# Batches of 4, 4, 3, 3 and 2 units, moved bias products, unread matmuls in waits, and no barrier between the samples and the experts

## What is computed

```python
qkv = src @ in_proj_w.T + in_proj_b
attn = softmax(einsum('sbhd,tbhd->bhst', q, k) * scale)   # over the samples
x = ln(src + (attn @ v) @ out_w.T + out_b)
probs = softmax(x @ gate_w.T + gate_b)
topv, topi = top_k(probs, 2)
for e in range(8):
    h = relu(tok @ w1[e].T + b1[e]) @ w2[e].T + b2[e]
    moe_out = moe_out + combine[:, e:e+1] * h
return ln(x + moe_out)
```

## Time and profile before

| | |
|---|---|
| time of 3 runs | 1171.24 us median (1170.41 to 1176.53) |
| the profiled execution | 1174.04 us, span 1172.3 us |
| mean granted TensorE clock | 0.971 |
| PE busy | 1103.8 us, 94% |
| DVE, POOL, ACT busy | 774.1, 522.6, 430.1 us |
| chain that ended last | PE 53%, issue 21%, DVE 14%, ACT 5%, POOL 4%, DMA 2% |

### The profile page before, as it was taken

How to read it: one execution, slowest core, us unless ns; L and a number is a source line. 1 busy time by engine, 2 the same in 40 slices (tenths; PEclk the granted TensorE clock), 3 DMA queues, 4 the chain that set the end, 5 groups by cost and what they waited for, 6 DMA issues and landing times.

```text
span 1172.3 us, 21067 instructions
## 1 busy us (share of the span) xinstructions
PE 1103.8 (94%) x7531; PEld 927.0 (79%) x7531; DVE 774.1 (66%) x1711; ACT 430.1 (37%) x890; POOL 522.6 (45%) x505
## 2 busy tenths in 40 slices
PE   9999999999899997999987999999999989989997
PEld 5888888886777765988986999999998678775565
DVE  5899889998887546888851222222222898887785
ACT  3545533335556411121112222222222455553466
POOL 6554224447776121768766111100254756531343
PEclk9999999999999997999977999999999999998999
DMA  6999700001000110000045422311221200000001
GB/s 221 398 394 388 265 1 1 19 7 71 17 1 1 28 75 1 1 2 28 34 143 201 158 108 107 108 38 38 63 81 39 62 10 10 1 1 2 0 28 46
DMA packets 44182, 93.61 MB, mean 80 GB/s; under 512 B 3885, under 2 KB 17998, under 8 KB 41414
## 3 DMA queue, kind: packets, MB, share of 16 engines
q1 hardware_dynamic: 35702, 62.24, 14.8%
q0 software_dynamic: 7104, 29.14, 6.9%
q10 hardware_dynamic: 1296, 1.18, 0.3%
HBM read 39.02 MB, written 51.51 MB: 77 GB/s over the span
## 4 chain that ended last, share of the span: by engine, by line
PE 53%; issue 21%; DVE 14%; ACT 5%; POOL 4%; DMA 2%; POOLq 1%; SPq 1%; PEldq 0%; DVEq 0%; PEld 0%; ACTq 0%
PE PS L2393 11%; PE PS L2403 11%; PE PS L1100 6%; PE PS L1078 3%; PE PS L1113 3%; PE PS L1068 2%; DVE scr L1459 2%; PE PS L1633 2%; PE PS L1026 2%; DVE scr L1485 2%; PE PS L1795 1%; POOL big L686 1%; DVE big L1372 1%; PE PS L1107 1%; PE PS L1023 1%
## 5 line engine op out<-in xcount | busy, mean ns | idle before, releaser
L2426 ACT ACTIVATE scr<-PS,W 128x128 f32<-128x128 f32 x148 | 53.5, 367 | 192.0 <-PE PS L2393 190.9
L2393 PEld LDWEIGHTS PS<-scr 128*128 128x128 f32 x992 | 118.2, 194 | 5.0 <-issue 1.8
L2393 PE MATMUL PS<-scr 128*128 128x128 f32 x992 | 120.2, 279 | 1.3 <-ACT scr L2421 1.3
L2403 PE MATMUL PS<-scr 128*128 128x256 f32 x496 | 112.2, 379 | 0.0
L718 POOL TENSOR_TENSOR scr<-scr,small 128x1232 f32<-128x1232 f32 x32 | 72.0, 2251 | 81.3 <-DVE small L469 81.0
L2456 DVE TENSOR_SCALAR scr<-PS,W 128x128 f32<-128x128 f32 x148 | 51.3, 350 | 82.2 <-PE PS L2393 82.2
L2403 PEld LDWEIGHTS PS<-scr 128*128 128x128 f32 x496 | 91.8, 190 | 11.2
L859 ACT ACTIVATE big<-PS 128x512 f32<-128x512 f32 x144 | 73.7, 524 | 73.0 <-PE PS L1078 72.6
L2462 DVE TENSOR_TENSOR scr<-PS,W 128x256 f32<-128x256 f32 x37 | 15.7, 425 | 125.6 <-PE PS L2403 118.3
L1100 PEld LDWEIGHTS PS<-scr,big 128*128 128x128 f32 x640 | 81.0, 191 | 8.1 <-issue 5.1
L1078 PE MATMUL PS<-W,scr 128*128 128x128 f32 x480 | 77.5, 280 | 10.1 <-ACT big L837 3.0
(11 more groups left out here) (418 smaller groups left out, 2500.4 us busy)
## 6 DMA issues: line engine op xcount, KB each, us to landing
expert_in<-zeros SPq DMA_DIRECT2D x1, 19712.0 KB, 61.8
expert_out<-zeros SPq DMA_DIRECT2D x1, 19712.0 KB, 112.8
scr<-ew_in POOLq DMA_DIRECT2D x12, 1024.0 KB, 6.4
scr<-expert_in SPq DMA_DIRECT2D x38, 128.0 KB
big<-ew_in POOLq DMA_DIRECT2D x4, 1024.0 KB, 8.3
expert_out<-scr POOLq DMA_DIRECT2D x28, 128.0 KB, 2.0
W<-pack SPq DMA_DIRECT2D x1, 2458.0 KB, 8.6
W<-pack SPq DMA_DIRECT2D x1, 2152.0 KB, 8.2
```

The costliest lines, as they stand in the source:

```text
L2393: ins = pe.matmul(bank(1 + f % 4, G), e_w1[slot][:, k, f * P:(f + 1) * P], e_xT[:, k, :], start=(k == 0), stop=(k == C - 1))
L2403: ins = pe.matmul(bank(5 + t, D), e_h[:, f, t * P:(t + 1) * P], e_w2[slot][:, f, :], start=(f == 0), stop=(f == FC - 1))
L2426: a.activation(e_h[:, f, :], bank(1 + f % 4, G), ACT.Relu, bias=moe_bias(e, f)).then_inc(s["h_act"], 1)
```

## The change

It moves the borders of three batches; rewrites the rounds in which units are scattered; makes the copy of `x_row8` in the stage "qkv" and over all 128 partitions; makes two bias parts before round 0, two inside the waits of rounds 17 and 19 and two at the end, each in a bank of its own; adds unread products in front of round 0 (16), in rounds 7, 11 and 14 (9 each), behind the samples (20) and in the tail's round 1 (7); lets SP read its registers before it waits for the scatters; and replaces the barriers behind "samp" (and PE's behind "qkv") by waits for `slot_ready` or `bias_taken`.

```diff
-        x_row8 = cut(E * P, parts=E).rearrange("p (e n) -> p e n", e=E)
+        x_row8 = cut(E * P).rearrange("p (e n) -> p e n", e=E)
...
@@ qkv_dve @@
             qkv_stats(v, ch, B - 1)
+            v.tensor_copy(x_row8, ident[:, 0:E].unsqueeze(2).broadcast_to([P, E, P])).then_inc(samp["row8_ready"], 1)
+            ch.inc(v.memset(x_run[:, 0, :], 0.0))
             v.wait_ge(s["rstd_ready"], B)
...
-        BATCHES = [(0, 4), (4, 8), (8, 12), (12, 14), (14, 16)]
+        BATCHES = [(0, 4), (4, 8), (8, 11), (11, 14), (14, 16)]
...
-        SCATTERED = {8: (0,), 9: (1,), 10: (2,), 11: (3,), 12: (4,), 13: (5,), 14: (6, 7), 15: (8,), 16: (9, 10), 17: (11, 12), 18: (13,),
-                     19: (14, 15)}
+        SCATTERED = {8: (0,), 9: (1,), 10: (2,), 11: (3,), 12: (4,), 13: (5, 6, 7), 14: (8,), 15: (9, 10), 17: (11, 12, 13), 19: (14, 15)}
...
-        BIAS_BANKS = (0, 1, 2, 3, 2, 3)
+        BIAS_BANKS = (6, 7, 0, 1, 2, 3)
+        EARLY_BIAS = 2
+        BIAS_IN = {UNITS + 1: 2, UNITS + 3: 3}
+        EB2_BANKS = (6, 7, 5, 4)
...
@@ bias_products @@
-            if n >= 4:
-                pe.wait_ge(bias_taken, n - 1)
...
@@ samp_dve @@
-            v.tensor_copy(x_row8, ident[0:E, 0:E].unsqueeze(2).broadcast_to([E, E, P])).then_inc(s["row8_ready"], 1)
-            ch.inc(v.memset(x_run[:, 0, :], 0.0))
...
@@ samp_pool @@
+                for u in SCATTERED.get(it, ()):
+                    scattered(u)
                 if it == UNITS:
...
                     weights_load(g, 0, 0)
-                for u in SCATTERED.get(it, ()):
-                    scattered(u)
...
@@ samp_act @@
             values_loaded(0)
+            for n, b in enumerate(EB2_BANKS):
+                a.wait_ge(s["eb2_psum"], n + 1)
+                a.activation(e_b2[:, (b - 4) * 512:(b - 3) * 512], bank(b), ACT.Copy).then_inc(s["eb2_kept"], 1)
             exps(0)
...
+            for n in range(EARLY_BIAS):
+                bias_kept(a, n, BIAS_BANKS[n])
...
-                if it > UNITS:
-                    bias_kept(a, it - UNITS - 1, BIAS_BANKS[it - UNITS - 1])
+                if it in BIAS_IN:
+                    bias_kept(a, BIAS_IN[it], BIAS_BANKS[BIAS_IN[it]])
...
@@ samp_pe @@
+            for b in EB2_BANKS:
+                if b == 4:
+                    pe.wait_ge(qkv["v_evac"], T + NT)
+                for e in (2 * (b - 4), 2 * (b - 4) + 1):
+                    ins = pe.matmul(bank(b, D, (e % 2) * D), x_row8[:, e, :], w["eb2"], start=True, stop=True)
+                ins.then_inc(s["eb2_psum"], 1)
+            pe.wait_ge(rows_zeroed, 16 * 9)
+            for n in range(EARLY_BIAS):
+                pe.wait_ge(s["eb2_kept"], n + 1)
+                bias_products(pe, n, BIAS_BANKS[n])
             pe.wait_ge(s["eb2_kept"], 4)
+            clocked(pe, 4, 16)
             for it in range(LAST + 1):
                 u, x, q = it - 1, it - 3, batch_at(it, 4)
+                if q is not None and it < UNITS:
+                    pe.wait_ge(s["xT_ready"], x)
+                    clocked(pe, 7, 9)
                 if 0 <= x < UNITS:
                     turned(x)
+                if it in BIAS_IN:
+                    bias_products(pe, BIAS_IN[it], BIAS_BANKS[BIAS_IN[it]])
                 if it:
+                    if it == 1:
+                        pe.wait_ge(bias_taken, EARLY_BIAS)
...
-                if it == UNITS:
-                    pe.wait_ge(rows_zeroed, 16 * 9)
-                if it >= UNITS:
-                    bias_products(pe, it - UNITS, BIAS_BANKS[it - UNITS])
-            for n in range(LAST + 1 - UNITS, len(BIAS_PARTS)):
+            for n in range(EARLY_BIAS + len(BIAS_IN), len(BIAS_PARTS)):
                 bias_products(pe, n, BIAS_BANKS[n])
             pe.sem_inc(moe["xT_psum"], 1)
+            clocked(pe, 4, 20)
+            pe.wait_ge(bias_taken, len(BIAS_PARTS))
...
@@ moe_sp @@
             sp.wait_ge(samp["slot_ready"], len(BATCHES) + 1)
-            sp.wait_ge(rows_moved, 16 * 2 * NT)
             def body(n, slot, e, ahead):
+                sp.wait_ge(rows_moved, 16 * 2 * NT)
                 sp.wait_ge(moe["xT_psum"], n + 1)
...
@@ moe_pe, moe_act, moe_dve, moe_pool: before the first register @@
+            pe.wait_ge(samp["slot_ready"], len(BATCHES) + 1)
...
@@ tail_pe @@
+                if j == 1:
+                    pe.wait_ge(*at("os_ready", 2))
+                    clocked(pe, 6, 7)
                 if 1 <= j <= B:
                     turn("f", j - 1)
...
@@ the engines' programs @@
-            stage_end(g, "samp")
+            stage_left(g)
-            stage_end(a, "samp")
+            stage_left(a)
-            stage_end(pe, "qkv")
+            stage_left(pe)
-            stage_end(pe, "samp")
+            stage_left(pe)
-            stage_end(v, "samp")
+            stage_left(v)
```

More of the change, by code:

```diff
@@ L2219, in samp_act @@
             values_loaded(0)
+            for n, b in enumerate(EB2_BANKS):
+                a.wait_ge(s["eb2_psum"], n + 1)
+                a.activation(e_b2[:, (b - 4) * 512:(b - 3) * 512], bank(b), ACT.Copy).then_inc(s["eb2_kept"], 1)
             exps(0)
-            for n in range(4):
-                a.wait_ge(s["eb2_psum"], n + 1)
-                a.activation(e_b2[:, n * 512:(n + 1) * 512], bank(4 + n), ACT.Copy).then_inc(s["eb2_kept"], 1)
+            for n in range(EARLY_BIAS):
+                bias_kept(a, n, BIAS_BANKS[n])
             for it in range(LAST + 1):
@@ L2242, in samp_act @@
                     a.activation(x_dif[:, 0:n, :], x_dif[:, 0:n, :], ACT.Exp).then_inc(s["texp_ready"], 1)
-                if it > UNITS:
-                    bias_kept(a, it - UNITS - 1, BIAS_BANKS[it - UNITS - 1])
-            for n in range(LAST - UNITS, len(BIAS_PARTS)):
+                if it in BIAS_IN:
+                    bias_kept(a, BIAS_IN[it], BIAS_BANKS[BIAS_IN[it]])
+            for n in range(EARLY_BIAS + len(BIAS_IN), len(BIAS_PARTS)):
                 bias_kept(a, n, BIAS_BANKS[n])
```

7 lines of the change are left out of this document (3 added, 4 removed).

## The result

The changed kernel takes 1166.71 us (median of 12 runs, 1163.53 to 1170.45), the kernel before beside it 1175.51 (12 runs, 1170.41 to 1179.97). The ratio is 0.9926, 95% interval 0.9908 to 0.9943: 0.7% faster, where 1157.0 (1.2%) had been forecast with a range of 1152 to 1166. The profiled executions are 1174.04 before (span 1172.3) and 1164.59 after (span 1162.9): 9.4 us.

The account below looks back on a forecast made before the run. PE was taken to bound mid-samples, with waits for DVE lowering its clock, and POOL's scatters and SP's registers the samples' end. Rounds 8.2, scatters 2.5, SP 2.6, tail 1.1, less 0.3 for the copy: 14.1 off 1171.24, 1157 us; range 1152 to 1166.

Parts of the forecast that it names:

- the third batch: Rounds 13 and 14: ending with unit 10 removes a 2.47 us wait and slow clock (1.7), fill loses 2.0; net 2.2 us.
- DVE and POOL don't take this back: Rounds 7 and 11: clock gains of 1.7 and 3.3 us stay, as next values were ready when PE needs them.
- The forecast's 134.2: Last qkv product to end of the samples' last sums: 142.4 us before, with a forecast gain of 8.2.
- Rival C: Rounds 13 and 14: six scatters in a row delay semaphores, costing 22 us against 14.1 won, 1179; chance 0.04.
- the samples' end: From last sums to first expert rows turned: forecast gain 5.1 us, from a shorter scatter row and SP's early registers.
- PE's end work ... lies in front of it and is done: Behind the samples: 24 bias and 20 unread products, 4.5 us at full clock, finish before the first expert rows arrive.
- SP has its registers by then and pays 0.2: Samples' end: SP reads registers before the last scatter lands, then pays 0.2 us for the issue instead of 2.79.
- The registers' 2.6: Samples' end: SP's early register reads bring the first rows in 2.6 us earlier.
- the shorter row's 2.5: Samples' end: ten scatters left in POOL's last row instead of 14 bring the first rows in 2.5 us earlier.
- Rival A: Samples' end: `GROUPS` stays 7.3 us behind the last slots, SP's reads follow, rows in at 614.6; 1160.7 us; chance 0.17.
- rival D: Experts: the second wait grows by what the first gives, at most 7.03 us more, 1164; chance 0.08.
- Rival B: Unread products don't hold the clock or stand in the way: rounds give -3.5 instead of 8.2, 1169.6 us; chance 0.07.

Follow-up runs that it names:

- run without fills: Changed kernel without the nine unread products in each of rounds 7, 11 and 14; median 1165.81 us, ratio to the kernel before 0.9944.
- two and two: Changed kernel, but round 13 scatters units 5 and 6 and round 14 units 7 and 8; 1161.07 us, one execution.
- old batches: Changed kernel with batches of 4, 4, 4, 2, 2 and the scatter rounds of the kernel before; median 1165.21 us, ratio to before 0.9920.
- even row: Changed kernel with scatters spread: none in round 12, two units each in 13 to 15, unit 10 in 16; median 1162.98 us, ratio to before 0.9908.
- row of eight: Changed kernel with unit 4 scattered in round 13 too, eight scatters in a row, none in round 12; 1165.72 us, one execution.
- one weight later: Changed kernel, but POOL loads expert 2's weights only behind its two additions; median 1166.29 us, ratio to before 0.9934.
- weights between: Even row without round 14's unread products, expert 2's weights loaded between POOL's two additions; median 1162.10 us, ratio to before 0.9892.

## Why the prediction was wrong

**Right.** The start gained 1.0, round 7 1.7 and round 11 3.0 (3.3 forecast), and the clock behind both picks is 1.00; the run without fills has 0.57 and 0.82 there. It loses 1.7 us in round 7 and 1.3 more until the end of round 11, so only 1.3 of round 11's 3.0 are shown to come from its fill; where the clock falls to without one differs between executions (0.64 before, 0.82 here). The bias parts, the experts' products and 16 unread ones fit in the start at no cost. The tail gained 1.04 (1.1). Scatters follow each other as forecast, and SP reads early. The copy in "qkv" cost 0 instead of 0.3: the qkv products take 44.59 us in both traces. Beside the copy, which ran at 406.53 to 407.19, POOL's first operation took 0.55 instead of 0.19 us. The Trainium skill, "SBUF — State Buffer", section "Who interferes with whom", has such a copy lock GpSimd out until it ends. The trace agrees: POOL's operation ended 0.05 us behind the copy. It cost POOL 0.36 us and TensorE nothing.

**The step that failed first** is the third batch, "net 2.2", and with it "DVE and POOL don't take this back". The rounds behind round 11 lost 2.2: at the end of round 11's sums 5.7 us had been gained against Q, at the end of the rounds 3.5. That is 4.4 us off the sum. I had weighed DVE's work against TensorE's and had not followed POOL through rounds 12 and 13. What the runs put in its place, in the order in which the edits took it away:
- Six scatters in a row in round 13, and in round 14 a count of TensorE's late by 2.5 us. Gone in two and two (2.5 us). This part was late in four of six executions of the same order, so whether a given execution pays it is chance; without it the sum is 0.3 gained behind round 11, still 1.9 off.
- POOL's product of unit 15, needed in round 13, which stands behind the scatters of unit 4 in round 12. TensorE waits 1.47 us for it; gone when nothing is scattered in round 12 (1.7 us). The old batches have this wait too, so it belongs to the gains of rounds 0 to 11, which POOL takes back in part, and not to the new batches.
- Nine unread products in round 14: counted at 2.0, they cost 0.9 where the rest was mended.

Taken from 138.9, these 5.1 us (2.5 + 1.7 + 0.9) leave 133.8, and 133.7 to 133.8 was measured in four executions. The forecast's 134.2 was within reach with the scatters spread evenly (134.7) and without the fill of round 14, not in the order that the change has.

Rival C named the first of these, six scatters in a row that delay counts in rounds 13 and 14, and gave it 22 us and a chance of 0.04. The mechanism was there, at 2.5 us: one count was late, and it cost 2.5 us and not 8.

**The second step that failed** is the samples' end, 3.5 instead of 5.1. "PE's end work ... lies in front of it and is done" was wrong, by my own rows: 24 bias products of 1.98 / 16 = 0.124 us and 20 unread ones of 0.225 are 7.5 us at full clock, not 4.5, and at the low clock they took 5.47 + 6.92 = 12.4. They began at 604.22 instead of about 601, since the rounds ended late and DVE's ranks with them. So TensorE, not the rows, set T. "SP has its registers by then and pays 0.2" failed too: the reads lasted until 612.9 and released the load, which was one of the forecast's own signs of being wrong. The registers' 2.6 were 1.7 at SP, the shorter row's 2.5 were 2.1 where the rows land, and behind TensorE's work they gave 0.8 and 1.2 at T, from one execution each. They don't add up to the 3.5; how the rest divides was not measured. Rival A, that the registers would be the end, came half true: `GROUPS` was ready 3.2 us behind the last slots (608.49 and 605.28) instead of 7.3, the slower reads set the landing of the rows, and TensorE's work hid it by 0.9 us.

In the experts 0.8 us were gained between T and the third turn where I had taken 0: the first products run at full clock (3.83), and the wait for the third rows gives about half of it back, rival D in small. Rival B is refuted in rounds 0 to 15 and in the tail by the clock rows; at the samples' end the unread products ran at a low clock and stood in the way, as it has it.

## What to carry to other kernels

When work is moved on a queue, write out that queue's whole order in the rounds it leaves and enters, and ask of each neighbour who waits for it: here the price was in a scatter that had not been moved. Sum the filler work in front of a hand-over at the clock that it will run at, not only the work it replaces. And measure each part of a compound change alone: three fills whose sum couldn't be told from nothing in the median were two that gained 3.0 us in their rounds and one that cost 0.9.

## What the runs showed of the hardware

- **Two SBUF operands.** DVE's operations on a unit's 128x128 scores (L2013 and L2020) take 0.29 us when one operand is in PSUM, also beside POOL's product (0.29 at 558.72 with POOL busy from 557.99). With both in SBUF they take 0.29 alone (once 0.36) and 0.36 to 2.92 beside such a product of 4.5 us, always until 0.15 us after it ends (1.93, 1.22 and 2.92 in the changed kernel, 1.74 and 1.68 before, 0.36 in the even row). The Trainium skill says so in "SBUF — State Buffer", section "Who interferes with whom": a VectorE instruction with two SBUF inputs contends with a GpSimd one that reads SBUF. The traces agree for POOL's long products; beside its short root (528.04 to 528.59 after) the 0.29 stood. I had cited the section for the copy and had not looked at the operands of the operations on the path.
- **Counts during rows of scatters.** A count raised by TensorE arrived 2.5 us (row of six) and over 3 us (row of eight) after its product's end, and at the samples' end ACT waited 9.12 us, until 613.00, for counts of bias products that in other executions of the same order came in time (608.41 in the kernel with one weight later). It isn't settled what decides it. The same order gives both.
- **Rows beside weights.** 128 KB of rows took 2.03 us alone and 7.80 beside 4 MB of weights (7.03 before). The Trainium skill, "DMA: Bandwidth & Descriptors", section "Queues, rings and completion order", says that each DMA engine takes turns between its queues a packet at a time; that fits, but no run here separates it from other causes. Whoever starts the weights sooner delays the rows, and the reverse costs the weights.
- **The clock.** A wait of 0.4 to 1.0 us left it at 1.00 (rounds 7, 11, 14); the waits of 2.3 and 2.7 us of the run without fills brought it to 0.57 and 0.82 over the work behind them. Before, the wait of 2.47 us gave 0.78. But the length of the wait alone doesn't decide: the changed kernel's 1.47 us in round 13 and 2.22 in round 15 left the clock at 1.00 over the 5.5 and 6.0 us behind them, and so did 2.42 us in the row of eight, while 2.21 us in the experts (weights between) brought 0.50 over the next 2.9. No run here separates what does.
